# Loading the weights of a recommender tower in thirteen pieces between the table loads

## The chip, the cores and the metric

The kernel runs on one core of a Trainium2 chip. The metric is the device time of one execution, in microseconds. The times are the median and the extremes of the runs shown; the profile comes from one further execution.

## The reference

For 512 samples, 26 embedding rows of 128 numbers are looked up in 26 tables (`tbl_0` to `tbl_25`, 1,000 to 125,000 rows). Together with the dense features they give 27 vectors a sample. All dot products of pairs of these vectors (351) and the dense features go through a small network of three layers:

```python
sd = jnp.einsum('bfd,bd->bf', sparse_values, dense_features)
ss = jnp.einsum('bfd,bgd->bfg', sparse_values, sparse_values)
pairs = ss[:, iu, ju]
z = jnp.concatenate([dense_features, sd, pairs], axis=1)
...
h = jnp.concatenate([z, r_dense_features], axis=1)
h = jnp.maximum(h @ W_top1 + b_top1, 0.0)
h = jnp.maximum(h @ W_top2 + b_top2, 0.0)
y = h @ W_top3
```

All of it is in float32.

## The kernel before, in words

The 512 samples are four tiles of 128. The six tables of 1,000 rows (`HOT`) are not gathered: each is loaded whole into SBUF, and a product of a one-hot matrix with the table picks the rows for all 512 samples. The other 20 tables are gathered by GpSimd with one indirect DMA for each table and tile, 80 in all, in six batches a tile.

**Picking stage (before the tiles).** For each hot table i, TensorE spreads the ids over the partitions (`spread_ids`, line 279, counted by `s_ps_ids`). DVE (line 455) and ACT (lines 568 and 580) turn them into one-hot rows. ACT rounds the table to a high part (`round_table`, line 557, counted by `s_hi`), DVE forms the low part (line 462, counted by `s_lo`), and TensorE multiplies both (`pick`, line 291, counted by `s_picked`). Between picks TensorE transposes the gathered rows of tile 0 (line 322, counted by `s_tp`), and DVE and ACT copy them into `vecs` (lines 474 and 542).

**The queue on SP.** SP issues the ids, tables 0 and 1 and the dense features at once. Table i from 2 on is issued when `s_hi` has reached i - 1, that is when table i - 2 has been rounded; the tables go through a ring of four buffers, so tables 4 and 5 also wait for `s_lo`. Each table is two DMAs (lines 222 and 223), of 112 and of 13 partitions. When the fifth table has been rounded (`s_hi` at 5), the six weight arrays are issued one after the other without a wait between them (lines 236 to 241): `w1_dense` 512 KB, `w1_dots` 1,536 KB, `b1`, `w2` 512 KB, `b2` and `w3`. The first three count on `s_w1`, the last three on `s_w2`. The last DMA of SP writes the output.

**Who waits for the weights.** DVE waits for `s_w1` and adds the two halves of `w1_dense` into `w1_fold` (line 482). TensorE waits for `s_w1`, `s_w2` and the fold, and then begins the dense part of tile 0 (`dense_part`, line 331). ACT waits for both before its first tile (line 598). TensorE starts the gram products of tile 0 (line 360) when ACT has placed the picked vectors (line 593, counted by `s_early`).

**A tile.** TensorE forms the gram products in four parts (line 360). DVE and ACT fold each part out of PSUM into `dots` (lines 498, 501, 505 on DVE, 610, 613, 617 on ACT); both wait for TensorE's count `s_gram`. Then come the products with `w1_dots` (line 378), the relu of layer 1 (lines 512 and 624, after `s_h1_dve` and `s_h1_act`), layer 2 (line 390), its relu, and layer 3 (line 338). Between these, TensorE transposes the rows of the next tile. Tile 0 and the last stand alone, tiles 1 and 2 are a loop. While the tiles run, GpSimd gathers the rows of later ones.

Of the kernel before, what the change touches and what calls it, by code (L numbers as in the profile page):

```python
# [54 lines left out]
NHOT = len(HOT)  # L55
# [25 lines left out]
PER_BANK = P // QUADS // PARTS // BANKS  # L81
BANK = 512
FOLD_DVE, FOLD_ACT = [0, 1], [2, 3]


def build(nc, ins, out):
    with ExitStack() as ctx:
        def sb(name, shape, dt=F32):
            return ctx.enter_context(nc.sbuf_tensor(name, shape, dt))
# [4 lines left out]
        def sem(name):  # L94
            return ctx.enter_context(nc.semaphore(name))
# [8 lines left out]
        w1_dense = sb("w1_dense", [P, 2, H1])  # L104
        w1_fold = sb("w1_fold", [P, H1])
        w1_dots = sb("w1_dots", [P, STEPS, H1])
        w2 = sb("w2", [P, OC1, H2])
        w3 = sb("w3", [P, OC2])
        b1 = sb("b1", [P, OC1])
        b2 = sb("b2", [P, OC2])  # L110
# [28 lines left out]
        s_hot_ids = sem("s_hot_ids")  # L139
        s_table = [sem(f"s_table{i}") for i in range(NHOT)]  # L140
        s_w1 = sem("s_w1")
        s_w2 = sem("s_w2")
        s_zero = sem("s_zero")
        s_ident = sem("s_ident")
        s_row_id = sem("s_row_id")
# [7 lines left out]
        s_hi = sem("s_hi")  # L153
# [61 lines left out]
        @block.sync  # L215
        def _(sp):
            def load_table(i):
                whole = ins[f"tbl_{HOT[i]}"].rearrange("(p k) d -> p k d", k=KT)
                if i >= TABLE_RING:

                    sp.wait_ge(s_lo, i - TABLE_RING + 1)
                sp.dma_start(table[0:KP_A, i % TABLE_RING], whole[0:KP_A]).then_inc(s_table[i], 16)
                sp.dma_start(table[KP_A:KP, i % TABLE_RING], whole[KP_A:KP]).then_inc(s_table[i], 16)

            sp.dma_start(ids[:, :, :], ins["ids"].rearrange("(p t) f -> p t f", t=TILES)).then_inc(s_ids, 16)
            sp.dma_start(hot_ids[:, :], ins["hot_ids"]).then_inc(s_hot_ids, 16)
            load_table(0)
            sp.dma_start(dense[:, :, :], ins["r_dense_features"].rearrange("(p t) d -> p t d", t=TILES)
                         ).then_inc(s_dense, 16)
            load_table(1)  # L230

            for i in range(2, NHOT):
                sp.wait_ge(s_hi, i - 1)
                load_table(i)
            sp.wait_ge(s_hi, NHOT - 1)
            sp.dma_start(w1_dense[:, :, :], ins["w1_dense"]).then_inc(s_w1, 16)
            sp.dma_start(w1_dots[:, :, :], ins["w1_dots"]).then_inc(s_w1, 16)
            sp.dma_start(b1[:, :], ins["b_top1"]).then_inc(s_w1, 16)
            sp.dma_start(w2[:, :, :], ins["W_top2"]).then_inc(s_w2, 16)
            sp.dma_start(b2[:, :], ins["b_top2"]).then_inc(s_w2, 16)  # L240
            sp.dma_start(w3[:, :], ins["W_top3"]).then_inc(s_w2, 16)

            sp.wait_ge(s_y_read, TILES)
            sp.dma_start(out.rearrange("(p t) o -> p (t o)", t=TILES), y[:, :]).then_inc(s_out, 16)
            sp.wait_ge(s_out, 16)
# [25 lines left out]
        def _(pe):  # L271
# [11 lines left out]
            def pick(i):  # L283

                pe.wait_ge(s_hi, i + 1)
                if i >= 2:

                    pe.wait_ge(s_pick_read, i - 1)

                def products(k, part):  # L290
                    return pe.matmul(ps_pick[:, i % 2, :], part[0:KP, i, k, :], one_hot[0:KP, i % RING, k, :],  # L291
                                     start=(part is table_hi and k == 0), stop=(part is table_lo and k == KT - 1))

                for k in range(KT):
                    if k == KT // 2 and i + 2 < NHOT:
                        spread_ids(i + 2)
                    if k in KS_ACT[i]:
                        pe.wait_ge(s_hot_act, steps_made(KS_ACT, i, KS_ACT[i].index(k) + 1))
                    for n, (k0, _) in enumerate(RUNS_DVE[i]):
                        if k == k0:  # L300
                            pe.wait_ge(s_hot_dve, steps_made(RUNS_DVE, i, n + 1))
                    products(k, table_hi)

                    if k == 1:
                        pe.wait_ge(s_lo, i + 1)
                        products(0, table_lo)
                    if k >= 1:
                        last = products(k, table_lo)
                last.then_inc(s_picked, 1)
# [107 lines left out]
                    for g in range(2 * i - 2, min(2 * i, NB)):  # L417
                        transposes(0, g)
            pe.wait_ge(s_pad, 2)
            pe.wait_ge(s_w1, 48)  # L420
            pe.wait_ge(s_w2, 48)
            pe.wait_ge(s_w1_fold, 1)
            dense_part(0, ps_h_dve, 0, s_h_dve_read)

# [10 lines left out]
        def _(dve):  # L435
# [42 lines left out]
            for g in range(2 * (NHOT - 3), NB, 2):  # L478
                read_transposed(0, g)

            dve.wait_ge(s_w1, 48)
            nc.vector.tensor_add(w1_fold[:, :], w1_dense[:, 0, :], w1_dense[:, 1, :]).then_inc(s_w1_fold, 1)
            dve.wait_ge(s_w2, 48)

            def read_y(t):
                dve.wait_ge(s_y, t + 1)
# [40 lines left out]
        def _(act):  # L527
# [67 lines left out]
            read_picked(NHOT - 1)  # L595

            act.wait_ge(s_pick_read, NHOT)
            act.wait_ge(s_w1, 48)
            act.wait_ge(s_w2, 48)

            def act_tile(t, following=True):
                def read_next(*batches):
# [78 lines left out]
```

## Time and profile before

| | us |
|---|---|
| median of 3 runs | 134.19 |
| lowest and highest | 133.56, 215.45 |
| the profiled execution, span | 178.9 |
| tile 0, from its first gram product to that of tile 1 | 25.0 |
| TensorE busy in the profile | 127.8 |
| ACT, DVE, GpSimd busy in the profile | 86.8, 79.5, 78.4 |

Of the profiled execution's own time the record holds the span, from its first instruction to its last; what lies around the span is not recorded. Engines: PE is TensorE's products and PEld its weight loads, DVE is VectorE, ACT ScalarE, POOL GpSimd, SP the engine that issues the plain DMAs (SPq is its queue). A row of the timeline has the start, the duration, the engine, the line of the kernel, the operation and how many were merged; in brackets stand the idle time of that engine before it and what ended it. "Remote" and "another core or an unknown queue" mean that the profile found no releaser; "issue" means that the engine waited for nothing that the profile shows. A wait for several counts is put down to the one that came last.

### The profile page before, as it was taken

The page shows a single profiled execution, that of the slowest core. Times are in us where ns is not written, and L with a number is a line of the kernel's source. Part 1 is how long each engine was busy: PE and PEld are TensorE (multiplying, and loading weights), DVE is VectorE, ACT ScalarE, POOL GpSimd, SP SyncE. Part 2 cuts the span into 40 slices and gives each one's busy share as a digit, 9 for nine tenths or more (in the row PEclk, how much of TensorE's full clock was granted, in tenths as well). Part 3 has the DMA queues.
Part 4 walks back from the last instruction along what each step waited for, and adds up shares of the span by engine and source line. Part 5 has one row for each costly group of instructions (what it writes and reads, how often), then busy time and mean ns, then how long its engine had stood idle before and what let it go on. Part 6 is the DMA issues. An engine that isn't in the chain of part 4 may idle for free.

```text
span 178.9 us, 2260 instructions
## 1 busy us (share of the span) xinstructions
PE 127.8 (71%) x752; PEld 112.7 (63%) x752; DVE 79.5 (44%) x217; ACT 86.8 (49%) x240; POOL 78.4 (44%) x87
## 2 busy tenths in 40 slices
PE   2499996236994986968450799685343999887794
PEld 1357764113883985967450799675333999877793
DVE  3799850008960498042402770050408623389201
ACT  4679916007971499530502766030508672289210
POOL 4777777735777005757771027477740000000000
PEclk9999999755799699999876558999555569999699
DMA  4985543980212001111211002111210000000000
GB/s 132 243 189 165 150 130 67 375 295 16 60 46 59 16 0 29 48 38 50 59 44 29 4 0 59 44 44 44 59 44 0 0 0 0 5 0 0 0 4 0
DMA packets 4801, 11.39 MB, mean 64 GB/s; under 512 B 2244, under 2 KB 2244, under 8 KB 4664
## 3 DMA queue, kind: packets, MB, share of 16 engines
q1 hardware_dynamic: 2232, 6.03, 11.3%
q0 software_dynamic: 2560, 5.25, 11.1%
q8 instruction: 5, 0.08, 0.2%
q14 instruction: 4, 0.03, 0.1%
HBM read 11.27 MB, written 0.00 MB: 63 GB/s over the span
## 4 chain that ended last, share of the span: by engine, by line
PE 35%; another core or an unknown queue 32%; DVE 17%; issue 5%; ACT 5%; DMA 3%; SPq 1%; ACTq 0%; DVEq 0%
PE ps_gram L291 11%; PE ps_h_bank L378 8%; DVE dots L501 7%; PE ps_gram L360 7%; DMA dense<-in_r_dense_features 3%; ACT dots L613 3%; DVE vecs L474 3%; PE ps_dve L322 2%; DVE dots L505 2%; PE ps_act L322 2%; PE ps_gram L390 2%; DVE dots L498 2%; PE ps_h_bank L331 1%; DVE one_hot L455 1%
## 5 line engine op out<-in xcount | busy, mean ns | idle before, releaser
L265 POOL DMA_INDIRECT rows<-in_tbl,ids_sb x80 | 77.6, 970 | 53.1 <-issue 22.6
L360 PE MATMUL ps_gram<-vecs 128*128 128x104 f32 x256 | 39.6, 323 | 27.2 <-ACT dots L617 17.9
L360 PEld LDWEIGHTS ps_gram<-vecs 128*128 128x128 f32 x256 | 37.6, 235 | 29.3 <-DVE dots L505 19.0
L378 PE MATMUL ps_h_bank<-dots,w_dots 128*128 128x128 f32 x192 | 26.2, 305 | 3.4 <-DVE dots L505 1.8
L378 PEld LDWEIGHTS ps_h_bank<-dots,w_dots 128*128 128x128 f32 x192 | 26.0, 222 | 3.7 <-DVE dots L505 3.7
L455 DVE TENSOR_TENSOR one_hot<-ps_gram,row_id 125x1024 fp32r<-125x1024 f32 (+1 forms) x18 | 19.0, 1098 | 17.2 <-remote 15.1
L291 PE MATMUL ps_gram<-one_hot,table_hi 125*128 125x512 f32 x48 | 22.0, 480 | 2.5 <-issue 2.3
L613 ACT COPY dots<-ps_gram 32x48 f32<-32x48 f32 x96 | 22.9, 239 | 1.3
L501 DVE COPY dots<-ps_gram 32x48 f32<-32x48 f32 x96 | 22.8, 238 | 1.6
L498 DVE COPY dots<-ps_gram 32x16 f32<-32x16 f32 x32 | 5.7, 177 | 39.9 <-remote 26.0
L610 ACT COPY dots<-ps_gram 32x16 f32<-32x16 f32 x32 | 5.8, 182 | 34.5 <-remote 26.0
L291 PE MATMUL ps_gram<-one_hot,table_lo 125*128 125x512 f32 x48 | 20.8, 455 | 1.7 <-issue 1.6
L542 ACT COPY vecs<-ps_act 128x512 f32<-128x512 f32 (+1 forms) x12 | 10.1, 840 | 21.3 <-remote 13.4
L512 DVE TENSOR_SCALAR h<-ps_h_bank,b 128x128 f32<-128x128 f32 x8 | 2.4, 347 | 30.2 <-remote 16.7
L568 ACT ACTIVATE distance<-ps_h_bank,minus_row_id 125x512 f32<-125x512 f32 x16 | 10.0, 698 | 11.4 <-remote 11.4
L291 PEld LDWEIGHTS ps_gram<-one_hot,table_hi 125*128 125x128 f32 x48 | 10.7, 230 | 7.4 <-issue 5.5
L291 PEld LDWEIGHTS ps_gram<-one_hot,table_lo 125*128 125x128 f32 x48 | 10.9, 228 | 4.6 <-issue 2.2
L474 DVE COPY vecs<-ps_dve 128x512 f32<-128x512 f32 (+1 forms) x12 | 11.8, 981 | 2.5 <-PE ps_act L322 1.6
L390 PE MATMUL ps_gram<-h,w 128*128 128x128 f32 x64 | 8.3, 278 | 2.8 <-DVE h L512 2.8
L390 PEld LDWEIGHTS ps_gram<-h,w 128*128 128x128 f32 x64 | 7.6, 192 | 3.1 <-DVE h L512 3.1
L322 PE MATMUL ps_dve<-ident,rows 128*128 128x128 f32 x44 | 8.1, 310 | 1.6 <-DVE vecs L474 1.5
L580 ACT ACTIVATE one_hot<-distance 125x512 fp32r<-125x512 f32 x16 | 9.1, 647 | 0.0
(41 smaller groups left out, 101.0 us busy)
## 6 DMA issues: line engine op xcount, KB each, us to landing
table<-in_tbl SPq DMA_DIRECT2D x6, 448.0 KB
w_dots<-in_w_dots SPq DMA_DIRECT2D x1, 1536.0 KB
rows<-in_tbl,ids_sb POOLq DMA_INDIRECT x80
w_dense<-in_w_dense SPq DMA_DIRECT2D x1, 512.0 KB
w<-in_W_top SPq DMA_DIRECT2D x1, 512.0 KB
table<-in_tbl SPq DMA_DIRECT2D x6, 52.0 KB
dense<-in_r_dense_features SPq DMA_DIRECT2D x1, 256.0 KB, 5.3
ids_sb<-in_ids SPq DMA_DIRECT2D x1, 52.0 KB, 1.9
```

The costliest lines, as they stand in the source:

```text
L265: pool.indirect_dma_start(out=rows[:, slot - EARLY, :], out_offset=None, in_=ins[f"tbl_{f}"], in_offset=bass.IndirectOffsetOnAxis(ap=ids[: ...
L291: return pe.matmul(ps_pick[:, i % 2, :], part[0:KP, i, k, :], one_hot[0:KP, i % RING, k, :], start=(part is table_hi and k == 0), stop=(pa ...
L322: last = pe.transpose(bank[:, k, :], rows[:, s0 - EARLY + k, :], ident[:, :])
L360: last = pe.matmul(ps_gram[:, part % 2 * BANKS + g // PER_BANK, c0:c0 + COLS], vecs[:, p0:p0 + QUADS, :], vecs[:, p0:p0 + QUADS, 1:SLOTS], ...
L378: last = pe.matmul(bank[:, o, :], w1_dots[:, j, (o0 + o) * P:(o0 + o + 1) * P], dots[:, j, :], start=False, stop=(j == STEPS - 1), skip_gr ...
L390: last = pe.matmul(bank, w2[:, c, o * P:(o + 1) * P], h1[:, c, :], start=(c == 2), stop=(c == 1))
L455: nc.vector.tensor_tensor(one_hot[0:KP, i % RING, k0:k1, :], ps_ids[0:KP, i % 2, :].unsqueeze(1).to_broadcast(shape), row_id[0:KP, k0:k1]. ...
L474: nc.vector.tensor_copy(slots_block(g), ps_dve[:, 0:BATCHES[g][1], :]).then_inc(s_dve_read, 1)
L501: nc.vector.tensor_copy(dst, src)
L542: nc.scalar.copy(slots_block(g), ps_act[:, 0:BATCHES[g][1], :]).then_inc(s_act_read, 1)
L568: nc.scalar.activation(distance[0:KP, n, :], ps_h_bank[0:KP, i % 2, :], ACT.Abs, bias=minus_row_id[0:KP, k:k + 1]).then_inc(s_distance, 1)
L613: nc.scalar.copy(dst, src)
```

## The change

The weights are no longer issued at the end. They are cut into thirteen pieces: the two halves of `w1_dense`, the six steps of `w1_dots`, two halves of `w2` (each of these ten is 256 KB, 2 KB to a partition), and `b1`, `b2` and `w3`. The order begins with `b1`. Each piece but the first is issued only when the one before it has landed. The first six stand between the loads of tables 2, 3, 4 and 5, the other seven behind table 5. One semaphore counts all pieces, and all engines that use weights wait for all thirteen.

```diff
-            for i in range(2, NHOT):
-                sp.wait_ge(s_hi, i - 1)
-                load_table(i)
-            sp.wait_ge(s_hi, NHOT - 1)
-            sp.dma_start(w1_dense[:, :, :], ins["w1_dense"]).then_inc(s_w1, 16)
-            sp.dma_start(w1_dots[:, :, :], ins["w1_dots"]).then_inc(s_w1, 16)
-            sp.dma_start(b1[:, :], ins["b_top1"]).then_inc(s_w1, 16)
-            sp.dma_start(w2[:, :, :], ins["W_top2"]).then_inc(s_w2, 16)
-            sp.dma_start(b2[:, :], ins["b_top2"]).then_inc(s_w2, 16)
-            sp.dma_start(w3[:, :], ins["W_top3"]).then_inc(s_w2, 16)
+            def weight_piece(n, dst, src):
+
+                if n >= 1:
+                    sp.wait_ge(s_w1, 16 * n)
+                sp.dma_start(dst, src).then_inc(s_w1, 16)
+
+            sp.wait_ge(s_hi, 1)
+            load_table(2)
+            weight_piece(0, b1[:, :], ins["b_top1"])
+            weight_piece(1, w1_dense[:, 0, :], ins["w1_dense"][:, 0, :])
+            sp.wait_ge(s_hi, 2)
+            load_table(3)
+            weight_piece(2, w1_dense[:, 1, :], ins["w1_dense"][:, 1, :])
+            weight_piece(3, w1_dots[:, 0, :], ins["w1_dots"][:, 0, :])
+            sp.wait_ge(s_hi, 3)
+            load_table(4)
+            weight_piece(4, w1_dots[:, 1, :], ins["w1_dots"][:, 1, :])
+            weight_piece(5, w1_dots[:, 2, :], ins["w1_dots"][:, 2, :])
+            sp.wait_ge(s_hi, 4)
+            load_table(5)
+            weight_piece(6, w1_dots[:, 3, :], ins["w1_dots"][:, 3, :])
...
+            weight_piece(8, w1_dots[:, 5, :], ins["w1_dots"][:, 5, :])
+            weight_piece(9, w2[:, 0:2, :], ins["W_top2"][:, 0:2, :])
+            weight_piece(10, w2[:, 2:4, :], ins["W_top2"][:, 2:4, :])
+            weight_piece(11, b2[:, :], ins["b_top2"])
+            weight_piece(12, w3[:, :], ins["W_top3"])
...
-            pe.wait_ge(s_w1, 48)
-            pe.wait_ge(s_w2, 48)
+            pe.wait_ge(s_w1, 16 * W_PIECES)
...
-            dve.wait_ge(s_w1, 48)
+            dve.wait_ge(s_w1, 16 * W_PIECES)
             nc.vector.tensor_add(w1_fold[:, :], w1_dense[:, 0, :], w1_dense[:, 1, :]).then_inc(s_w1_fold, 1)
-            dve.wait_ge(s_w2, 48)
...
-            act.wait_ge(s_w1, 48)
-            act.wait_ge(s_w2, 48)
+            act.wait_ge(s_w1, 16 * W_PIECES)
```

On SP, from the load of table 2 to the end, this stood before. The names are those of the kernel without their numbers: `w_dense` is `w1_dense`, `w_dots` is `w1_dots`, `b` is `b1` and then `b2`, `w` is `w2` and then `w3`.

```order
L222 DMA table<-in_tbl 112x1024 [waits s_lo,s_hi]
L223 DMA table<-in_tbl 13x1024
L236 DMA w_dense<-in_w_dense 128x1024 [waits s_hi]
L237 DMA w_dots<-in_w_dots 128x3072
L238 DMA b<-in_b_top 128x4
L239 DMA w<-in_W_top 128x1024
L240 DMA b<-in_b_top 128x2
L241 DMA w<-in_W_top 128x2
L244 DMA out_y<-y 128x4 [waits s_y_read]
```

These rows are the last table load and all that followed it. After the change, from the load of table 2 on, SP has the following; line 236 is now the issue within `weight_piece`.

```order
L222 DMA table<-in_tbl 112x1024 [waits s_hi]
L223 DMA table<-in_tbl 13x1024
L236 DMA b<-in_b_top 128x4
L236 DMA w_dense<-in_w_dense 128x512 [waits s_w1]
L222 DMA table<-in_tbl 112x1024 [waits s_hi]
L223 DMA table<-in_tbl 13x1024
...
L236 DMA w_dots<-in_w_dots 128x512 [waits s_w1] x3
L236 DMA w<-in_W_top 128x512 [waits s_w1] x2
L236 DMA b<-in_b_top 128x2 [waits s_w1]
L236 DMA w<-in_W_top 128x2 [waits s_w1]
L261 DMA out_y<-y 128x4 [waits s_y_read]
```

Every piece but the first has a wait for `s_w1` ahead of it, and the load of table 3 now stands behind one such wait; those of tables 4 and 5 stand behind two more each. On PE, at the passage from the last pick to tile 0, this stood before.

```order
L291 MATMUL ps_gram<-one_hot,table_hi 128x512 [waits s_hot_dve]
L291 MATMUL ps_gram<-one_hot,table_lo 128x512
L331 MATMUL ps_h_bank<-early,w_fold 128x128 [waits s_w2,s_w1_fold,s_w1,s_pad]
L331 MATMUL ps_h_bank<-early,w_fold 128x128
L360 MATMUL ps_gram<-vecs 128x104 [waits s_act_read,s_dve_read,s_early]
```

After the change the same place has the same instructions, with line numbers that are 17 higher.

```order
L308 MATMUL ps_gram<-one_hot,table_hi 128x512 [waits s_hot_dve]
L308 MATMUL ps_gram<-one_hot,table_lo 128x512
L348 MATMUL ps_h_bank<-early,w_fold 128x128 [waits s_w1_fold,s_w1,s_pad]
L348 MATMUL ps_h_bank<-early,w_fold 128x128
L377 MATMUL ps_gram<-vecs 128x104 [waits s_act_read,s_dve_read,s_early]
```

Nothing moved on PE: only the wait for `s_w2` went into the longer count of `s_w1`.

## Rows read from the trace of the kernel before

**Rows 1.** The head of the profile's page.
```profile
span 178.9 us, 2260 instructions
```

**Rows 2.** Busy time by stretch, the four tiles; the ends: PEclk, DMA share, GB/s.
```profile
57.02:82.06 25.04, 20.39 (x156) 19.31 (x157) 12.95 (x46) 15.11 (x49) 10.24 (x11) 0.93 0.12 30
82.06:119.43 37.37, 24.93 (x160) 24.03 (x160) 12.75 (x47) 14.49 (x48) 18.81 (x21) 0.77 0.13 36
119.43:155.00 35.57, 24.69 (x161) 24.04 (x161) 12.79 (x47) 14.54 (x48) 9.64 (x11) 0.71 0.08 21
155.00:178.90 23.90, 18.41 (x140) 17.68 (x140) 10.28 (x45) 10.11 (x43) 0.00 (x0) 0.93 0.01 1
```

**Rows 3.** The list of waits: us in total, times, the longest.
```profile
DVE dots L498 <- remote: 26.0, 4, 9.0
...
ACT vecs L593 <- remote: 3.4, 1, 3.4
```

**Rows 4.** Timeline, PE and DVE in tile 0: start, us, engine, line.
```profile
70.26 5.60 PE L378 MATMUL ps_h_bank<-dots,w_dots 128*128 128x128 f32 x48 [1.61 <-ACT dots L617]
...
78.47 0.61 DVE L512 TENSOR_SCALAR h<-ps_h_bank,b 128x128 f32<-128x128 f32 x2 [7.48 <-remote]
```

**Rows 5.** Timeline of PE, ACT and DVE in the picking stage.
```profile
24.43 0.39 PE L279 MATMUL ps_h_bank<-hot_ids_r,ones_row 6*128 6x512 f32 x1
...
26.38 1.05 ACT L542 COPY vecs<-ps_act 128x512 f32<-128x512 f32 x1 [3.65 <-remote]
...
39.71 0.58 PE L291 MATMUL ps_gram<-one_hot,table_hi 125*128 125x512 f32 x1 [0.81 <-issue]
...
40.41 0.59 PE L291 MATMUL ps_gram<-one_hot,table_lo 125*128 125x512 f32 x1
...
41.15 1.23 DVE L455 TENSOR_TENSOR one_hot<-ps_gram,row_id 125x1024 fp32r<-125x1024 f32 x1 [15.11 <-remote]
41.21 1.84 ACT L568 ACTIVATE distance<-ps_h_bank,minus_row_id 125x512 f32<-125x512 f32 x3 [11.38 <-remote]
...
45.77 1.07 ACT L557 CAST table_hi<-table 125x1024 fp32r<-125x1024 f32 x1
...
51.51 0.69 DVE L482 TENSOR_TENSOR w_fold<-w_dense 128x512 f32<-128x512 f32 x1
...
53.58 0.39 PE L291 MATMUL ps_gram<-one_hot,table_lo 125*128 125x512 f32 x1
...
57.02 1.31 PE L360 MATMUL ps_gram<-vecs 128*128 128x104 f32 x7 [2.60 <-issue]
```

**Rows 6.** Timeline of SP's queue: tables 2 to 5 and the first weights.
```profile
7.00 0.31 SPq L222 DMA_DIRECT2D table<-in_tbl  x1
...
11.58 0.31 SPq L222 DMA_DIRECT2D table<-in_tbl  x1
...
15.81 0.31 SPq L222 DMA_DIRECT2D table<-in_tbl  x1
...
20.53 0.31 SPq L222 DMA_DIRECT2D table<-in_tbl  x1
20.89 0.40 SPq L223 DMA_DIRECT2D table<-in_tbl  x1
29.86 0.35 SPq L236 DMA_DIRECT2D w_dense<-in_w_dense  x1
```

**Rows 7.** DMA view of 24 to 45 us: GB/s in 40 slices of 0.525.
```profile
GB/s 39 109 16 47 78 0 125 0 109 16 31 117 8 164 328 351 429 437 351 374 421 367 398 398 298 244 383 391 306 189 39 8 0 0 0 0 117 8 0 0
```

**Rows 8.** DMA issues of the whole page: KB each, us from issue to landing.
```profile
dense<-in_r_dense_features SPq DMA_DIRECT2D x1, 256.0 KB, 5.3
...
out_y<-y SPq DMA_DIRECT2D x1, 2.0 KB, 1.4
```

**Rows 9.** DMA view of 7 to 12 us, then of 20 to 25: GB/s, slices of 0.125.
```profile
GB/s 295 229 295 230 197 295 230 230 98 295 164 197 197 295 295 164 328 197 164 229 229 164 229 262 393 197 262 230 328 164 164 164 197 230 131 66 99 0 66 0
...
GB/s 66 0 0 0 0 0 0 0 262 229 33 66 229 262 131 131 131 360 295 328 426 393 361 295 426 295 98 230 66 262 131 66 66 66 33 0 0 0 197 262
```

More of the change, by code:

```diff
@@ L83 @@
 FOLD_DVE, FOLD_ACT = [0, 1], [2, 3]
+W_PIECES = 13
 def build(nc, ins, out):
@@ L141, in build @@
         s_w1 = sem("s_w1")
-        s_w2 = sem("s_w2")
         s_zero = sem("s_zero")
@@ L230, in _ @@
             load_table(1)
-            for i in range(2, NHOT):
-                sp.wait_ge(s_hi, i - 1)
-                load_table(i)
-            sp.wait_ge(s_hi, NHOT - 1)
-            sp.dma_start(w1_dense[:, :, :], ins["w1_dense"]).then_inc(s_w1, 16)
-            sp.dma_start(w1_dots[:, :, :], ins["w1_dots"]).then_inc(s_w1, 16)
-            sp.dma_start(b1[:, :], ins["b_top1"]).then_inc(s_w1, 16)
-            sp.dma_start(w2[:, :, :], ins["W_top2"]).then_inc(s_w2, 16)
-            sp.dma_start(b2[:, :], ins["b_top2"]).then_inc(s_w2, 16)
-            sp.dma_start(w3[:, :], ins["W_top3"]).then_inc(s_w2, 16)
+            def weight_piece(n, dst, src):
[17 more added lines that the diff above has]
+            weight_piece(6, w1_dots[:, 3, :], ins["w1_dots"][:, 3, :])
+            weight_piece(7, w1_dots[:, 4, :], ins["w1_dots"][:, 4, :])
+            weight_piece(8, w1_dots[:, 5, :], ins["w1_dots"][:, 5, :])
[3 more added lines that the diff above has]
+            weight_piece(12, w3[:, :], ins["W_top3"])
             sp.wait_ge(s_y_read, TILES)
```

## The prediction, made before the changed kernel ran

> **What bounds the kernel now.** I first set the profile's own time beside the runs. The profiled execution has a span of 178.9 us [rows 1]; of its time outside the span the record shows nothing. The median of the runs shown is 134.19 us, 44.7 less, and the runs themselves are 133.56, 134.19 and 215.45. So before a stall of this profile is taken for the kernel's, it has to be asked whether an ordinary run can contain it.
>
> The view of busy time by stretch gives the four sample tiles [rows 2]. The work is the same in each: DVE 12.95, 12.75 and 12.79 us, ACT 15.11, 14.49 and 14.54 in tiles 0, 1 and 2. Yet they last 25.04, 37.37 and 35.57 us. The last tile, which transfers almost nothing (1 GB/s), lasts 23.90 with its output. The list of waits says what fills the long ones: DVE stood 26.0 us in four waits put down to "remote", ahead of its first fold of a part [rows 3]. A wait of that kind has no releaser that the profile knows; by the program it is a wait for PE's count, and PE's matmuls were over. Tile 0 shows one plainly: PE's last w1_dots product is over at 70.26 + 5.60 = 75.86, and DVE, which waits for that group, starts at 78.47 [rows 4].
>
> Next the timeline of the picking stage, in which the weights travel [rows 5]. Three things are to be seen. PE had spread the ids for one_hot 4 at 24.43 + 0.39 = 24.82, but ACT and DVE, which wait for just that, start at 41.21 and 41.15, after 11.38 and 15.11 us idle, again "remote". ACT had stood 3.65 us before 26.38 in the same way, ahead of the weights. And PE itself crawls, one product every 0.7 us (39.71, 40.41). SP's queue shows the weights issued from 29.86, once the fifth table is rounded [rows 6], and the transfer row for 24 to 45 us (slices of 0.525 us) shows some 300 to 437 GB/s from 31 us, ending at about 40.3 [rows 7]. All engines but POOL come back within 1 us of that end.
>
> Does an ordinary run have this? I take the stalls out one by one. Picking: ACT's 3.65 + 11.38 = 15.03, and PE's 2.60 before its first gram at 57.02, which is s_early late by ACT's wait of 3.4 [rows 3, 5]: 17.63. Tiles 1 and 2 beyond tile 0: 12.33 + 10.53. The stall inside tile 0 (78.47 - 75.86 = 2.61), once for each of the first three tiles: 7.83. Together 48.3, and 178.9 - 48.3 = 130.6. With the 15.03 left in, 145.6. The median is 134.19, and whatever lies around the span counts in it too. So the stall under the weights costs an ordinary run at most 134.19 - 130.6 = 3.6 us, and nothing if 3.6 lie around the span. I take it as nothing.
>
> What would make such a stall peculiar to a profiled run: the Trainium skill, "NOTIFIC — the notification-queue block", section 7.1, says that the block which collects the engines' event records holds back its producers when its internal path fills, and can so throttle an engine. The trace agrees in shape (signals late under traffic, work equal), but no row shows the block itself. By that rule the change shortens the profile and not the runs, which is my forecast.
>
> **The change, part by part.** An ordinary run's picking stage I get by moving rows 5 back by 15.03. DVE is ready for the fold of w1 at 51.51 - 15.03 = 36.5. PE ends its last pick at 53.58 + 0.39 - 15.03 = 38.94 and then wants w_fold (line 331). The weights before: issued at 29.86 less ACT's 3.65, 26.2; landed 10.4 later (29.86 to 40.3), 36.6; fold 0.69, and PE has it at 37.4, 1.5 before it asks. They bind nothing before, so an earlier start gains nothing.
>
> Removed: six issues in a row and the wait for the fifth rounding. Added on SP: twelve waits, each for the whole of the piece ahead. Behind them on SP stand the loads of tables 3, 4 and 5. Added on PE, ACT and DVE: all three now wait for thirteen landings before anything with weights; DVE's fold waited for w1's three only, which matters little, as PE waited for all six already.
>
> The price of a link. Fixed: the smallest DMA of the page, the 2 KB output, lands 1.4 us after its issue [rows 8]. Size: the last table load is issued in two parts, at 20.53 and 20.89, and the transfer row of 20 to 25 us runs to 24.4 [rows 6, 9]; 24.4 - 20.9 - 1.4 = 2.1 for the 500 KB of both among gathers, so some 1.1 for 256 KB: 2.5 us a piece. At the burst's best rate (437 GB/s, rows 7) it is 0.6, so 2.0. The dense load of 256 KB took 5.3 [rows 8], but with two table loads in the same queue. So 2.0 from below and 5.3 from above; I take x = 2.4, close to the table row, which ran among the same gathers. For the two tiny pieces at the end, y = 1.5, the output's 1.4 and a little for SP.
>
> The chain's end. Piece 0 is issued behind table 2 (7.00) and lands with it; the row of 7 to 12 us has that traffic over by 11.9 [rows 6, 9]. Call it 12.0. Ten pieces of 256 KB and two tiny ones follow, each issued when the one ahead has landed: C = 12.0 + 10x + 2y = 12.0 + 24 + 3 = 39.0. Pieces 2, 4 and 6 are issued behind a table load, some 1.5 us after it; a table takes 3.5 from its last issue, so it is in about 2 us after the piece's issue, and 2.4 just covers it. After the fold, PE may go at C + 0.69 + 0.1 = 39.8, against 38.94: about 0.9 us late. ACT's matching wait and s_early follow at the same time, so it goes into the end one to one.
>
> The tables. Table 3 goes out when piece 0 is in and piece 1 issued, at 12.5 instead of 11.58; table 4 at about 17.3 instead of 15.81; table 5 at about 22.3 instead of 20.53. With 3.9 from first issue to landing, table 5 lands at 26.2. ACT rounds it at 45.77 in the profile [rows 5], 30.7 in an ordinary run. Slack of 4 us: cost nothing. If x were 3.3 or more, that cover would begin to go.
>
> A gain is possible too: gathers of tile 0 no longer share the queues with a burst. It is bounded by the 3.6 us above, with everything else; I take zero.
>
> Sum: 134.19 + 0.9 = 135.1 us.
>
> **Rivals.** First, faster: part of the weight stall is in ordinary runs, and small pieces let signals through. For it: ACT, DVE and PE all stand exactly until the weights are in [rows 5, 7]. Against it: the sum leaves 3.6 us at most, and like stalls come at some 30 GB/s, without any weights [rows 2, 3]. Price: 134.19 - 3.6 = 130.6 if the chain is in by 38.1; the whole 15.03 would be 119.2, for which the rest of an ordinary run would have to be 11 us shorter than the trace without its stalls. Chance of more than 2% faster: 0.2.
>
> Second, slower: the chain ends late, PE stands at line 331 of the old numbering for w_fold. It decides from C + 0.8 - 38.94 = 2.7, which with y = 1.5 is x = 2.6, only 0.2 above my value. With x = 2.8, still well below the dense row's 5.3, C = 43.0 and the delay is 4.9: 139.0 us. For it: the chain never runs two pieces together, and gathers go on all the while. Against it: the later links have no table beside them. Chance: 0.3.
>
> The Trainium skill, "DMA: Bandwidth & Descriptors", speaks for this rival: its "Rules for kernel authors" say to coalesce, and "Anatomy of one DMA" fits 2.0 us fixed and bytes over 436 GB/s, measured on GpSimd's path. As an estimate from that page, a piece would be 2.6 and a tiny one 2.0, C = 42.0, and the time 134.19 + 3.9 = 138.1. The trace's 1.4 for a 2 KB store on SP's path [rows 8] is lower than its fixed part, so I stay with the rows.
>
> That the change does nothing to the profile either (the stall is not from the weights but falls there) has a small share of the middle case.
>
> **How the numbers follow.** Within 2%, 0.5: the chain lands between 2.7 us too late and early, and the stall is a matter of the profile. This case alone runs from 132.5 to 136.9. Faster 0.2, slower 0.3. The 2% is about what a measurement of this kernel can tell from no change. The range, 130.0 to 139.5, holds the faster case as far as the sum allows it and the slower one to x = 2.8; outside I leave a stall that was whole in ordinary runs and a chain with x of 2.9 and more.
>
> **What would show it.** In the changed kernel's profile: pieces issued from SP 2.0 to 2.6 us apart, the last tiny one landing at 38 to 40 us; no row above 350 GB/s for several us; ACT's wait of 11.4 before its distance gone or split; the span shorter by 10 us or more while the runs stay where they were. PE idle before the product with w_fold, for DVE's fold, would show the chain late and by how much. Wrong would be: runs below 130 (the stall was real in them), or pieces 3 us apart and runs above 139.

## The result, and the profile after

The changed kernel takes 141.72 us in the median of 4 runs (139.57 to 214.77), the kernel before 135.66 (133.56 to 215.45). The ratios in this document leave out the runs in the slower of the two states that the executions of a kernel fall into; here the ratio is 1.0435, with a 95% interval of 1.0335 to 1.0535: slower by some 4%. The forecast was 135.1 in a range of 130.0 to 139.5, so it was wrong: the time lies above the range, on the side of the second rival.

The profile of before that stands ahead of the prediction [rows 1] is from an execution 45 us longer than the ordinary ones; the comparisons below use a second profile of the same kernel, of 135.3 us (experiment 1). Around the span lie 1.9 us: the changed kernel's profiled run took 139.57 us, with this span.

```profile
span 137.7 us, 2264 instructions
```

Where the time went is told by the chain that ended last, here its part from the load of table 2 to the first tile; the columns are start, us, and what. Every step from 7.43 to 45.45 is a piece of the weights.

```profile
7.43 3.99 DMA b<-in_b_top
11.43 2.58 DMA w_dense<-in_w_dense
14.03 3.09 DMA w_dense<-in_w_dense
17.14 3.27 DMA w_dots<-in_w_dots
20.43 2.95 DMA w_dots<-in_w_dots
23.40 3.04 DMA w_dots<-in_w_dots
26.45 3.40 DMA w_dots<-in_w_dots
29.87 2.89 DMA w_dots<-in_w_dots
32.77 3.10 DMA w_dots<-in_w_dots
35.89 2.59 DMA w<-in_W_top
38.50 3.09 DMA w<-in_W_top
41.61 2.03 DMA b<-in_b_top
43.66 1.77 DMA w<-in_W_top
45.45 0.70 DVE w_fold L498
...
46.29 0.68 PE ps_h_bank L348 x4
46.97 2.95 PE ps_gram L377 x16
```

The ten pieces of 256 KB take 41.61 - 11.43 = 30.2 us, 3.0 each; the two tiny ones at the end 1.9 on average. The timeline of DVE and PE at the passage to tile 0, which answers to the end of [rows 5], shows who waits for them.

```profile
43.73 0.39 PE L308 MATMUL ps_gram<-one_hot,table_lo 125*128 125x512 f32 x1
...
45.45 0.69 DVE L498 TENSOR_TENSOR w_fold<-w_dense 128x512 f32<-128x512 f32 x1 [5.43 <-DMA w<-in_W_top]
...
46.29 0.68 PE L348 MATMUL ps_h_bank<-early,w_fold 128*128 128x128 f32 x4 [2.17 <-DVE w_fold L498]
46.81 5.34 PE L377 MATMUL ps_gram<-vecs 128*128 128x104 f32 x32
```

DVE has been done with its one-hots for 5.43 us when the last piece lands; PE has ended its last pick at 44.12 and stands 2.17 for the fold. The 11.38 and 15.11 us of idle ACT and DVE [rows 5] are gone, but they are gone from an ordinary run of the kernel before as well, as experiment 1 shows.

### The profile page after: what moved, and what is told of

It is laid out like the page before. It is cut to its first block, busy times and chain, and to the rows that moved or that the text cites. A ratio compares the mean times of both kernels' runs of the same rounds, so it can differ in the third digit from the quotient of the medians.

```text
span 137.7 us, 2264 instructions
## 1 busy us (share of the span) xinstructions
PE 111.1 (81%) x752; PEld 98.4 (71%) x752; DVE 79.4 (58%) x217; ACT 87.0 (63%) x240; POOL 80.0 (58%) x87
## 4 chain that ended last, share of the span: by engine, by line
PE 33%; DMA 30%; DVE 21%; ACT 7%; issue 4%; SPq 1%; ACTq 0%
PE ps_h_bank L395 17%; DMA w_dots<-in_w_dots 14%; DVE dots L516 11%; PE ps_gram L377 7%; DMA w<-in_W_top 5%; PE ps_gram L407 5%; DMA b<-in_b_top 4%; DMA w_dense<-in_w_dense 4%; ACT dots L627 4%; DVE dots L520 4%; DVE dots L513 3%; DMA table<-in_tbl 3%; DVE vecs L490 2%; PE ps_dve L339 2%; ACT dots L631 1%
## 5 line engine op out<-in xcount | busy, mean ns | idle before, releaser
L282 POOL DMA_INDIRECT rows<-in_tbl,ids_sb x80 | 79.2, 990 | 27.0 <-issue 23.8
L377 PE MATMUL ps_gram<-vecs 128*128 128x104 f32 x256 | 32.8, 286 | 6.2 <-ACT dots L631 2.7
L377 PEld LDWEIGHTS ps_gram<-vecs 128*128 128x128 f32 x256 | 31.1, 201 | 8.0 <-DVE dots L520 5.4
L395 PE MATMUL ps_h_bank<-dots,w_dots 128*128 128x128 f32 x192 | 24.0, 289 | 5.3 <-DVE dots L520 3.8
L395 PEld LDWEIGHTS ps_h_bank<-dots,w_dots 128*128 128x128 f32 x192 | 23.4, 204 | 6.0 <-DVE dots L520 6.0
L308 PE MATMUL ps_gram<-one_hot,table_hi 125*128 125x512 f32 x48 | 20.5, 449 | 0.0
L308 PE MATMUL ps_gram<-one_hot,table_lo 125*128 125x512 f32 x48 | 19.4, 425 | 0.0
L527 DVE TENSOR_SCALAR h<-ps_h_bank,b 128x128 f32<-128x128 f32 x8 | 2.4, 346 | 21.8 <-PE ps_h_bank L395 21.8
L308 PEld LDWEIGHTS ps_gram<-one_hot,table_hi 125*128 125x128 f32 x48 | 9.7, 210 | 3.7 <-issue 1.5
L339 PE MATMUL ps_act<-ident,rows 128*128 128x128 f32 x36 | 6.4, 291 | 5.3 <-DMA rows<-in_tbl,ids_sb 5.3
L339 PEld LDWEIGHTS ps_act<-ident,rows 128*128 128x128 f32 x36 | 4.6, 149 | 5.5 <-DMA rows<-in_tbl,ids_sb 5.5
```

The lines of the kernel that those rows point to most:

```text
L282: pool.indirect_dma_start(out=rows[:, slot - EARLY, :], out_offset=None, in_=ins[f"tbl_{f}"], in_offset=bass.IndirectOffsetOnAxis(ap=ids[: ...
L339: last = pe.transpose(bank[:, k, :], rows[:, s0 - EARLY + k, :], ident[:, :])
L377: last = pe.matmul(ps_gram[:, part % 2 * BANKS + g // PER_BANK, c0:c0 + COLS], vecs[:, p0:p0 + QUADS, :], vecs[:, p0:p0 + QUADS, 1:SLOTS], ...
L395: last = pe.matmul(bank[:, o, :], w1_dots[:, j, (o0 + o) * P:(o0 + o + 1) * P], dots[:, j, :], start=False, stop=(j == STEPS - 1), skip_gr ...
```

## The experiments

Two theories were set against each other. **Late chain**: thirteen pieces, one in flight, land too late, and all that is lost is lost at the wait for them. **Late gathers**: the pieces stand in the queues between the gathers of tile 0, and TensorE waits for the gathered rows; in the changed kernel's profile it did so for 5.3 us until 28.85. What each expects is given with numbers ahead of every run.

### 1. The kernel before, a second profile

No edit.

> The kernel before, unchanged, for a profile of an ordinary execution. Two theories of the 6 us that the change cost. Late chain: the pieces take 3.0 us each, so the weights land at 45.4 us, and all is lost at the wait for them. Late gathers: the pieces take the queues from the gathers of tile 0, whose rows made TensorE wait 5.3 us in the changed kernel. Late chain expects a wait for gathered rows of 4 us or more here too, and no wait at all for the weights. Late gathers expects that wait under 2 us and the last pick over by about 39 us. Both: span about 132 to 135, and the 15 us stall under the weights of the first profile gone or nearly so.

Measured: 135.3 us (kernel before beside it: 136.23 in the median of 7), span 133.3. The timeline of SP, ACT, PE and DVE:

```profile
25.17 1.83 ACT L568 ACTIVATE distance<-ps_h_bank,minus_row_id 125x512 f32<-125x512 f32 x3
...
25.29 0.35 SPq L236 DMA_DIRECT2D w_dense<-in_w_dense  x1
...
34.77 0.66 PE L322 MATMUL ps_dve<-ident,rows 128*128 128x128 f32 x4 [3.15 <-DMA rows<-in_tbl,ids_sb]
...
38.67 0.68 DVE L482 TENSOR_TENSOR w_fold<-w_dense 128x512 f32<-128x512 f32 x1
...
44.53 0.39 PE L291 MATMUL ps_gram<-one_hot,table_lo 125*128 125x512 f32 x1
44.77 0.61 PE L331 MATMUL ps_h_bank<-early,w_fold 128*128 128x128 f32 x4
45.39 3.82 PE L360 MATMUL ps_gram<-vecs 128*128 128x104 f32 x32
```

ACT forms its distance at 25.17 without idle time ahead of it, just as the weights are issued; the stall of 11.38 us is not there. Nobody waits for the weights: the fold at 38.67 follows DVE's last one-hot without idle time, and PE passes from its last pick to the fold's product and the grams without a gap. There is a wait for gathered rows, 3.15 us, under the burst of the weights. It lies between what the two theories expected (4 or more, under 2), so by itself it decides nothing between them.

The tiles of both, in the view of busy time by stretch as in [rows 2], first the kernel before:

```profile
45.39:67.16 21.77, 18.31 (x157) 17.58 (x157) 12.78 (x46) 14.96 (x49) 16.28 (x19) 1.00 0.21 52
67.16:89.03 21.87, 18.90 (x161) 18.10 (x161) 13.01 (x47) 14.78 (x48) 16.68 (x18) 1.00 0.22 55
89.03:110.84 21.81, 18.93 (x160) 18.09 (x160) 13.02 (x47) 14.78 (x48) 12.56 (x14) 1.00 0.16 42
110.84:133.30 22.46, 16.85 (x140) 16.08 (x140) 10.39 (x45) 10.22 (x43) 0.00 (x0) 0.98 0.01 2
```

Then the changed kernel's first profile:

```profile
46.81:69.63 22.82, 19.83 (x159) 19.10 (x157) 12.80 (x46) 14.56 (x48) 16.08 (x18) 0.93 0.19 50
69.63:91.33 21.70, 18.86 (x160) 18.09 (x161) 12.86 (x47) 14.61 (x48) 16.52 (x18) 1.00 0.21 55
91.33:112.92 21.59, 18.85 (x161) 18.09 (x161) 12.84 (x47) 14.57 (x48) 12.32 (x14) 1.00 0.16 43
112.92:137.70 24.78, 18.41 (x140) 17.71 (x140) 10.20 (x45) 10.01 (x43) 0.00 (x0) 0.90 0.01 2
```

The spans differ by 4.4 us: 1.42 at the start of tile 0 (46.81 against 45.39), 1.05 in tile 0, nothing in the middle (-0.39) and 2.32 in the last tile. In the first and the last tile TensorE's granted clock is lower (0.93 and 0.90, against 1.00 and 0.98). At the start of tile 0 the two profiles differ by less than the medians of the two kernels do (1.42 against some 6); one reason is that this run of before had lost time of its own ahead of it, the 3.15 us for rows.

### 2. Two pieces in flight

```diff
-                if n >= 1:
-                    sp.wait_ge(s_w1, 16 * n)
-                sp.dma_start(dst, src).then_inc(s_w1, 16)
+                s = s_w[n % 2]
+                if n >= 2:
+                    sp.wait_ge(s, 16 * (n // 2))
+                sp.dma_start(dst, src).then_inc(s, 16)
...
```

PE, DVE and ACT wait for all pieces on both counts, at the same places as in the changed kernel.

> The changed kernel with two pieces in flight instead of one, on two semaphores. Late chain: the weights land by 32 to 36 us, nobody waits for them, and the time goes back to within 2% of before (about 135 to 137). Late gathers: the same bytes stand beside the gathers, the wait for rows stays at 5 us or grows, and the time stays at 139 to 142.

Measured: 136.24 us (133.36 to 137.34) against 136.23 of before. The last piece was issued at 32.38, the fold came at 37.78 without a wait for a piece, the first gram at 42.42. TensorE's wait for rows was 3.3 us. The loss is gone with the same pieces at the same places of the queue, as late chain expected; late gathers expected 139 to 142.

### 3. The same transfers, waited for late

```diff
-            pe.wait_ge(s_w1, 16 * W_PIECES)
             pe.wait_ge(s_w1_fold, 1)
...
-            dve.wait_ge(s_w1, 16 * W_PIECES)
+            dve.wait_ge(s_w1, 16 * 3)
...
                 next_transposes(0, 1)
+                if first:
+                    pe.wait_ge(s_w1, 16 * W_PIECES)
```

ACT's wait is cut to three pieces in the same way, and DVE and ACT wait for all thirteen ahead of the first relu.

> The changed kernel, transfers as they are, but the engines wait late: for b1 and the two dense pieces before the fold, and for the rest only before the first products with w_dots in tile 0. The weights at 45 us are then in time. Late chain: the whole loss goes, 134 to 137. Late gathers: only the 2.2 us go that TensorE stood for the fold, 139 to 140.

Measured: 134.75 us (132.42 to 135.14) against 136.23. The last piece was issued at 45.26, as late as in the changed kernel, and it cost nothing. The transfers are those of the changed kernel, so the whole loss lies in the wait for them. The timeline of PE shows also why the earlier start does not give more:

```profile
40.24 0.40 PE L308 MATMUL ps_gram<-one_hot,table_lo 125*128 125x512 f32 x1
...
40.47 0.61 PE L348 MATMUL ps_h_bank<-early,w_fold 128*128 128x128 f32 x4
41.10 3.82 PE L377 MATMUL ps_gram<-vecs 128*128 128x104 f32 x32
...
106.29 0.65 PE L339 MATMUL ps_dve<-ident,rows 128*128 128x128 f32 x4 [1.78 <-DMA rows<-in_tbl,ids_sb]
```

Tile 0 begins at 41.10, 4.3 us ahead of experiment 1; at 106.29 TensorE waits for the rows of the last tile, for the first time since the picking stage.

### 4. The same pieces with no wait between them

```diff
-                if n >= 1:
-                    sp.wait_ge(s_w1, 16 * n)
                 sp.dma_start(dst, src).then_inc(s_w1, 16)
```

> The changed kernel without the waits between pieces: the same pieces at the same places of the queue, all in flight as they are issued. Late chain: weights in by about 32 us, time 134 to 137. Late gathers: the queues are fuller between 12 and 28 us than in the changed kernel, the rows later still, time 141 or more.

Measured: 136.19 us (135.56 to 138.85) against 136.23; the ratio is 1.0104 (1.0034 to 1.0173), so about 1% may remain. Here all pieces are issued ahead of 24 us, TensorE waits 2.0 us for rows, and the fold at 39.05 does not wait. Late gathers expected 141 or more. So most of the loss comes not from where the pieces stand in the queue but from each waiting for the one before.

### 5. Eight links instead of thirteen

```diff
-W_PIECES = 13
+W_PIECES = 8
...
+            weight_piece(1, w1_dense[:, :, :], ins["w1_dense"])
...
+            weight_piece(2, w1_dots[:, 0:2, :], ins["w1_dots"][:, 0:2, :])
...
+            weight_piece(3, w1_dots[:, 2:4, :], ins["w1_dots"][:, 2:4, :])
+            weight_piece(4, w1_dots[:, 4:6, :], ins["w1_dots"][:, 4:6, :])
+            weight_piece(5, w2[:, :, :], ins["W_top2"])
...
```

The lines of the old pieces go; `b2` and `w3` follow as pieces 6 and 7.

> The changed kernel with eight pieces instead of thirteen: w1_dense whole, w1_dots in three pieces of 512 KB, w2 whole, still one in flight and still between the tables. From the changed kernel's links (3.0 us for 256 KB, 1.9 for a tiny one) a link of 512 KB is 4.1, so the last lands at 12 + 5 x 4.1 + 2 x 1.9 = 36 us. Late chain: nobody waits for the weights, 134 to 137 us. Late gathers: the same bytes at the same places, 139 to 142.

Measured: 133.72 us (132.22 to 160.14) against 134.53 of before. DVE's row gives the end of the chain:

```profile
37.34 0.69 DVE L493 TENSOR_TENSOR w_fold<-w_dense 128x512 f32<-128x512 f32 x1 [1.57 <-DMA w<-in_W_top]
```

The weights are in at 37.3, where 36 was worked out; PE ends its picks at 41.6 and does not notice. One piece in flight, between the tables, costs nothing here with a chain of eight links.

### 6. Three links more

```diff
             weight_piece(12, w3[:, :], ins["W_top3"])
+            for n in (13, 14, 15):
+                weight_piece(n, spare_w3[:, :], ins["W_top3"])
...
```

`W_PIECES` is 16 here, so all three engines wait for these links too.

> The changed kernel with three more tiny links at the end of the chain (w3 loaded three times more into a buffer that nobody reads), for which all wait as well. Late chain: 3 x 1.9 = 5.7 us later, 145 to 148 us. Late gathers or a lost clock alone: no change against the changed kernel, 140 to 142.

Measured: 145.15 us in the median of 5 (144.05 to 150.34), ratio to before 1.0762 (1.0623 to 1.0902); the changed kernel on the same chip, experiment 8, has 142.29. In the profiled run, of 150.02 us (one of the two longest), the three links took from 50.38 to 55.75, 1.8 each, and this is what they do:

```profile
55.75 0.69 DVE L501 TENSOR_TENSOR w_fold<-w_dense 128x512 f32<-128x512 f32 x1 [15.69 <-DMA spare_w<-in_W_top]
...
56.59 1.20 PE L351 MATMUL ps_h_bank<-early,w_fold 128*128 128x128 f32 x4 [14.57 <-DVE w_fold L501]
```

The step is in the direction and, in the median, at the lower edge of what late chain expected: 2.9 us over experiment 8 where 5.7 were priced. The lowest times differ by 3.3. Why not the whole 5.4 shows in the medians was not followed up; the chains of single runs differ by about as much: table 2 with `b1` behind it was in at 11.4 us in the changed kernel's profile and at 13.6 in this one, and the piece ahead of the three links landed at 45.45 there and at 50.38 here.

### 7. The burst of before, begun after the gathers of tile 0

```diff
-            sp.wait_ge(s_hi, NHOT - 1)
+            sp.wait_ge(s_rows[NB - 1], 16 * BATCHES[NB - 1][1])
...
```

`b1` is issued ahead of `w1_dots`, and the waits for the weights are late, as in experiment 3.

> The kernel before, with its weights in one burst, but begun when the last gather of tile 0 has landed, and with late waits (the fold waits for w1_dense and b1, the rest is waited for before the first products with w_dots). If the burst delays the gathers of tile 0 (3.15 us of TensorE in the second profile of before), that wait goes and the first gram product comes at 40 to 42 instead of 45.4. GpSimd's 80 gathers then set the end: the last tile cannot begin before about 108, so 131 to 134 us, 1 to 3% below before. If the burst costs the gathers nothing, 134 to 136.

Measured: 136.17 us (133.63 to 137.07) against 134.53: no gain where 131 to 134 was expected, a miss. The stage did what was expected: no wait for rows, picks over at 39.3, first gram at 39.77, 5.6 us ahead of experiment 1. The end did not follow:

```profile
106.06 0.65 PE L322 MATMUL ps_dve<-ident,rows 128*128 128x128 f32 x4 [2.41 <-DMA rows<-in_tbl,ids_sb]
...
108.18 5.42 PE L360 MATMUL ps_gram<-vecs 128*128 128x104 f32 x32 [0.55 <-ACT vecs L543]
...
121.67 7.22 PE L380 MATMUL ps_h_bank<-dots,w_dots 128*128 128x128 f32 x48 [1.80 <-DVE dots L504]
```

TensorE waits 2.41 us for rows again, at the same place as in experiment 3, and the last tile begins at 108.18 here and at 108.35 there. GpSimd's last gather begins at 104.7 in this run and at 104.6 in experiment 1. GpSimd goes from each of its 80 gathers to the next, most of them 0.94 us and 0.30 of issue, and they set the earliest start of the last tile. That is half of it: the last tile still begins 2.7 us ahead of that of experiment 1 (108.18 against 110.84), and then takes 25.6 us against 22.46, as its first 32 grams take 5.42 us (3.82 there) and its 48 products with `w1_dots` 7.22 (5.60): TensorE's granted clock is 0.63 from 109 to 112.5 and 0.61 from 122.5 to 126. The gathers by themselves leave room for a gain: in experiment 5 the last tile begins at 107.98, these two groups take 3.79 and 5.60, and the span is 130.4.

### 8. The changed kernel, a second profile

> The changed kernel, unchanged, for a second profile on the same chip as the others. Late chain: the chain lands at 45 us or later again, DVE stands for it by 5 us or more ahead of the fold, and the time is 139 to 143. If the first profile's loss lay in TensorE's clock (half for 3.4 us in the last tile), that fall need not come again and the time can be 2 us lower with the chain as late.

Measured: 142.29 us (140.78 to 144.07), ratio 1.0552 (1.0379 to 1.0724). The passage to tile 0:

```profile
40.90 0.40 PE L308 MATMUL ps_gram<-one_hot,table_lo 125*128 125x512 f32 x1
...
46.52 0.69 DVE L498 TENSOR_TENSOR w_fold<-w_dense 128x512 f32<-128x512 f32 x1 [11.18 <-DMA w<-in_W_top]
...
47.36 1.20 PE L348 MATMUL ps_h_bank<-early,w_fold 128*128 128x128 f32 x4 [6.06 <-DVE w_fold L498]
48.35 5.38 PE L377 MATMUL ps_gram<-vecs 128*128 128x104 f32 x32
```

Here the gathers were quick, the picks were over at 41.30 (44.12 in the first profile), and the chain still ended at 46.5. So the 5.3 us for rows in the first profile were hidden behind the weights: here TensorE waits for the fold 3.9 us longer, 2.8 because the picks were over earlier and 1.1 because the chain ended later. Tile 0 begins at 46.81, 48.35 and 57.58 in the three profiles in which TensorE waits for a chain of thirteen or sixteen links with one in flight (this kernel's two and experiment 6), and between 39.77 and 43.70 in experiments 2, 3, 4, 5 and 7. This and experiments 2 to 5 settle it for late chain.

## Why the prediction was wrong, point by point

**That an ordinary run does not hold the 15 us stall: right.** Experiment 1 has neither idle time. The sum that took the stalls out came to 130.6; with the 2.0 us around the span that experiment 1 shows (135.3 - 133.3) it is 132.6, and the lowest run of before seen later is 132.81. Inside it two errors offset each other in part, which is luck: the last pick ends at 44.92 in experiment 1, not at 38.94, with 3.15 us for rows among the causes, and a tile takes 21.8 us, where 25.04 - 2.61 = 22.4 was used. What made the first profile stall was not tried and stays open; no run shows the block that the prediction named for it.

**That the weights bind nothing before: right.** The fold waits for no piece in experiment 1, and the earlier landings of experiments 2, 4 and 5 gain nothing that the runs can tell.

**The price of a link: this step failed.** "I take x = 2.4, close to the table row" and y = 1.5: the profile after has 3.0 and 1.9. C = 12.0 + 10x + 2y gives 12.0 + 30.2 + 3.8 = 46.0 with these, 39.0 was forecast, and 45.45 and 46.52 were measured. The form of the sum held, its two prices were too low; ten links turn 0.6 us into six. The end of the range for x was 5.3 and the delay at x = 3.0 could have been read from the same formula: 46.0 + 0.8 - 38.94 = 7.9, or 142.1 us. The range of the time stopped at x = 2.8 nevertheless. That 142.1 is so near the measured 141.72 is in part luck: the picks end at 44.12 and 41.30 in the two profiles, not at 38.94, TensorE stands for the fold 2.17 and 6.06 us, not 7.9, and its clock, which is not in the formula, makes up for part of the rest.

**Why a link costs more than the rows said** is seen in two transfer rows of the changed kernel, first of 41 to 46 us in slices of 0.125, then of 38 to 42 in slices of 0.1:

```profile
GB/s 49 115 33 0 33 0 164 229 131 0 0 66 1 3 4 2 164 229 98 0 33 0 0 0 0 0 197 164 66 68 37 3 0 0 0 0 131 262 98 33
...
GB/s 103 164 123 123 164 41 0 41 0 0 0 0 0 246 205 266 62 185 82 205 225 184 246 246 246 266 225 348 164 328 62 103 82 0 0 41 0 0 246 246
```

The tiny piece issued at 41.61 is the 1, 3, 4, 2 from 42.5 to 43.0: 0.9 us pass before its first byte, and after its last byte another 0.66 to the next issue at 43.66. The values of 98 to 262 in that row are gathers. The 256 KB issued at 38.50 have their first byte no earlier than 39.3, 0.8 later; they and the gathers beside them run to 41.3, 2.0 us, and the next issue follows 0.3 later. So some 2.0 of a link of 3.1 are bytes among gathers.

The forecast had 1.1 for these bytes because it misread its table row: it took 1.4, a time from issue to landing, off a time that ends with the last byte. The traffic of that row lasts from 21.0 to 24.4 [rows 9], up to 3.4 us for 500 KB or 1.7 for 256 KB; with the 1.4 that is up to 3.1 a link, an estimate from the forecast's own rows and beyond its point of decision at 2.6. Nor was the 1.4 of the output store [rows 8] a firm price for a tiny piece: the same store lands after 1.4 us in experiment 1 and after 2.3 in the changed kernel's first profile, and why was not followed up.

**The estimate from the Trainium skill** had 2.6 for a piece and 2.0 for a tiny one, from the fit of 2.0 us and bytes over 436 GB/s that the page gives for GpSimd's path (the Trainium skill, "DMA: Bandwidth & Descriptors", "Anatomy of one DMA"), and 138.1 us. The tiny pieces agree (1.9); the large ones are dearer still (3.0). The rule of the same page of the Trainium skill to coalesce small transfers ("Rules for kernel authors") agrees with experiment 5 beside experiment 8: 133.72 with eight links, 142.29 with thirteen.

**The tables: right.** Table 5 went out at 23.84 instead of the forecast 22.3, and ACT rounded it at 32.44 without waiting for it.

**One to one into the end: too little.** The wait cost more than its length: the first 32 grams take 5.34 and 5.38 us in the changed kernel's two profiles, 3.82 in experiment 1. The view of busy time has a granted clock of 0.50, the lower of the two levels (1.2 GHz), from 47.4 to 50.6, after TensorE had stood ahead of 46.29; the same stretch of the kernel before, 45.4 to 49.2, has 1.00. That is 1.5 us more, and the forecast had no term for it.

**The rivals.** The second was the one, with its mechanism, its place and its point of decision (x = 2.6), at 0.3; its price was too low for the reason above. The first (faster) is excluded: nothing in experiment 1 waits for the weights. What spoke for it was read too strongly: PE did not stand until the weights were in, it ran single products at 39.71 and 40.41 [rows 5].

## What to carry to other kernels

A chain of transfers with one in flight is priced link by link from the rows of a transfer among the same traffic: the time to its first byte, its bytes, and the time from the last byte to the next issue. Its uncertainty grows with the number of links: with ten of them, 0.6 us a link decided the sign. Shorten the chain or move the waits to where each piece is needed before giving up the throttle: eight links, two in flight, and late waits each took the whole loss away. And before a stage is shortened, look for the next floor: here the picking stage could end 5 us earlier than in experiment 1 and the last tile still began at 108 us, when the gathers were through.

## What the runs showed of the hardware that was not expected

TensorE's clock falls in the last tile as well. In the changed kernel's first profile the granted clock is 0.50 from 126 to 129 us, while TensorE runs the 48 products with w_dots, after it had stood 1.80 us for DVE's folds; the 48 take 7.22 us, against 5.60 in experiment 1, where the clock is 1.00 from 123 to 127 after a wait of 1.84. Experiments 2, 3, 4, 6, 7 and 8 have such a fall in the last tile, experiments 1 and 5 do not. It costs some 2 us (24.78 against 22.46 for the tile). Since experiments 2, 3, 4 and 7 have it without the loss, it does not come from the late chain; whether the kernel before has it in the last tile too, its one ordinary profile does not show. In most of that kernel's runs the clock does fall somewhere: of the fourteen timed beside the experiments the two shortest (132.81 and 133.46 us) have a mean granted clock of 1.00, the others 0.971 to 0.987. What decides it between runs that stand for equal times was not found.

The same kernel's gathers land quickly or late from run to run: the first batch that TensorE waited for in the picking stage came 5.29 us late in one profile of the changed kernel and 1.31 in the other.
